# Graph layer on one core: both degree factors folded into the fp16 matrix tiles, pairs 0 and 1 prepared during the counts

## What is computed

```
h = relu(layernorm(x))                     # over the 1024 columns
avg = mean of h over the 64 images; rows normalised; sim = (avg @ avg.T + 1)/2
adj[s,d] = sim + gumbel0 > 1 - sim + gumbel1         # 0/1, 1024 x 1024
nmask = clip(adj + adj.T + I, 0, 1); common = nmask @ nmask.T
W = adj * common**2 / common.max()         # where the pair is valid
deg = W.sum(axis=0); dinv = deg**-0.5 (0 where deg is 0)
Wn = dinv[:, None] * W * dinv[None, :]
out = x + (Wn applied to h, times w) + bias          # for each image
```

## Time and profile before

| | |
|---|---|
| median of 3 runs | 912.77 us |
| profiled execution, its own time | 917.18 us |
| its span | 915.3 us |
| mean granted TensorE clock | 0.978 |
| PE busy | 846.0 us, 92% |
| VectorE (DVE) busy | 748.9 us, 82% |
| ScalarE (ACT) busy | 424.2 us, 46% |
| POOL busy | 336.9 us, 37% |

### The profile page before, as it was taken

One profiled execution on the slowest core, in us unless ns is written; L12 is line 12 of the kernel. 1 busy time (PEld: TensorE's weight loads), 2 busy tenths in 40 slices (PEclk: granted clock), 3 DMA queues, 4 the chain that ended last, 5 costly groups with the idle time before them and its releaser, 6 DMA issues.

```text
span 915.3 us, 13816 instructions
## 1 busy us (share of the span) xinstructions
PE 846.0 (92%) x4772; PEld 435.1 (48%) x4772; DVE 748.9 (82%) x792; ACT 424.2 (46%) x472; POOL 336.9 (37%) x264
## 2 busy tenths in 40 slices
PE   5999899968999999999999999999999999999997
PEld 3444455654454445444444454444444444444453
DVE  7998666888888888888888888888888888888885
ACT  3888703455444443444344444444444444444431
POOL 4788511254333333333333333333334333433330
PEclk9999899868999999999999999999999999999999
DMA  8999600040222222222222232223222222222112
GB/s 351 409 399 401 278 1 1 1 184 1 92 93 93 92 92 92 92 92 92 106 94 94 94 135 89 98 94 113 92 92 92 92 92 92 92 92 92 47 47 92
DMA packets 29108, 109.40 MB, mean 120 GB/s; under 512 B 3360, under 2 KB 3488, under 8 KB 28064
## 3 DMA queue, kind: packets, MB, share of 16 engines
q1 hardware_dynamic: 29088, 109.13, 32.3%
HBM read 75.56 MB, written 33.55 MB: 119 GB/s over the span
## 4 chain that ended last, share of the span: by engine, by line
DVE 29%; issue 27%; PE 14%; ACT 14%; POOL 13%; DVEq 1%; ACTq 1%; POOLq 1%; DMA 0%; SPq 0%
DVE zbuf L920 8%; DVE obuf L932 7%; DVE obuf L962 5%; POOL zbuf L372 5%; ACT ybuf L462 4%; PE ps L683 4%; POOL zbuf L370 4%; PE ps L650 3%; ACT hring L447 3%; ACT hring L446 3%; DVE ybuf L928 2%; DVE obuf L966 2%; PE ps L555 2%; ACT p L476 1%; PE ps L626 1%
## 5 line engine op out<-in xcount | busy, mean ns | idle before, releaser
L683 PE MATMUL ps<-a,ybuf 128*128 128x512 f16 x2688 | 598.8, 380 | 36.3 <-ACT obuf L476 29.9
L683 PEld LDWEIGHTS ps<-a,ybuf 128*128 128x128 f16 x2688 | 256.6, 98 | 357.4 <-ACT obuf L476 50.5
L462 ACT ACTIVATE ybuf<-zbuf 128x1024 f16<-128x1024 f32 (+1 forms) x128 | 121.6, 950 | 333.3 <-DVE zbuf L920 227.8
L928 DVE TENSOR_TENSOR ybuf<-zbuf,ybuf 128x1024 f16<-128x1024 f32 (+1 forms) x128 | 190.0, 1484 | 60.3 <-ACT ybuf L462 60.3
L370 POOL TENSOR_TENSOR zbuf<-zbuf 128x512 f32<-128x512 f32 x32 | 41.5, 1296 | 455.3 <-DVE zbuf L920 455.3
L850 DVE TENSOR_TENSOR hring<-hring 128x1024 f16<-128x1024 f32 x56 | 73.3, 1308 | 51.3 <-ACT hring L447 51.3
L674 PE MATMUL ps<-w,hring 128*128 128x128 f16 x1344 | 85.5, 221 | 3.6 <-DVE hring L850 3.6
L674 PEld LDWEIGHTS ps<-w,hring 128*128 128x128 f16 x1344 | 79.6, 99 | 18.4 <-DVE zbuf L920 7.4
L476 ACT ACTIVATE obuf<-ps 128x512 f32<-128x512 f32 x96 | 56.2, 586 | 64.3 <-PE ps L683 64.3
L939 DVE SCALAR_TENSOR_TENSOR obuf<-obuf,bias_sb,xring 128x1024 f32<-128x1024 f32 x64 | 82.2, 1285 | 2.9
L375 POOL TENSOR_TENSOR zbuf<-zbuf 128x512 f32<-128x512 f32 x32 | 71.8, 2244 | 0.0
(11 more groups left out here) (142 smaller groups left out, 629.6 us busy)
## 6 DMA issues: line engine op xcount, KB each, us to landing
xring<-in_x_dram SPq DMA_DIRECT2D x96, 512.0 KB, 5.0
out_dram<-obuf SPq DMA_DIRECT2D x64, 512.0 KB, 3.0
ybuf<-in_x_dram SPq DMA_DIRECT2D x28, 512.0 KB, 9.7
a<-in_L_gnn_gumbel_dram SPq DMA_DIRECT2D x7, 1024.0 KB, 14.7
obuf<-in_x_dram SPq DMA_DIRECT2D x4, 512.0 KB, 11.8
obuf<-in_L_gnn_gumbel_dram SPq DMA_DIRECT2D x1, 1024.0 KB, 22.9
w<-in_adj_dram SPq DMA_DIRECT2D x1, 64.0 KB, 1.8
bias_sb<-in_L_gnn_bias_dram SPq DMA_DIRECT2D x1, 0.5 KB, 2.1
```

Of the source, the lines that this page charges most:

```text
L462: nc.scalar.activation(y16[:, q % 2, 0, a:a + n, :], z[:, a + 1:a + 1 + n, :], ACT.Copy).then_inc(s_yhi, 1)
L683: mm = nc.tensor.matmul(bank[q % 2], y16[:, q % 2, yk, u, c * P:(c + 1) * P], a16[:, ak, mat, c, :], start=(start and c == yk == ak == 0), ...
L928: nc.vector.tensor_tensor(y16[:, q % 2, 1, a:a + n, :], z[:, a + 1:a + 1 + n, :], y16[:, q % 2, 0, a:a + n, :], ALU.subtract).then_inc(s_y, 1)
```

## The change

- **Factors.** `degree` is now the row sum of the squares of transposed masked counts: PE transposes `adjm` chunk by chunk (`turn_adj`), ScalarE copies the result out of PSUM (`turned`), VectorE multiplies the same counts with it (`mask_t`), ScalarE squares with an accumulated sum (`degree_of`). POOL raises the degrees to -1/4 (`roots`). The build multiplies the masked counts with that root of the row and of the column (`rooted`, eight tiles), and ScalarE squares with a scale `kappa` (`square`). So both factors are in the matrix, and a single factor `w_out` is left for the result.
- **Build.** t and high and low parts are now made for all four chunks of a matrix at once (2048 elements for each partition), in the order `MADE`. One of the t is POOL's (line 391). 
- **Pairs 0 and 1.** Their relu, x·W, z and y stand between the counts on all four engines. Images 1, 2 and 3 go to `obuf` as soon as `adjm` is done, the other loads of x wait for the matrices that lie in `xring`.
- **Loop.** `z_of` is a plain copy with a constant scale and moves from VectorE to ScalarE. `partial` keeps three of its four copies and adds scale and bias in them. VectorE's part is two multiply-adds for the upper halves, two for the lower and the add of x.

The diff, cut to its core:

```diff
-            sp.wait_ge(s_com, C)
-            sp.wait_ge(s_m, C)
-            for j in (1, 2, 3, 0, 4, 5, 6, 7):
+            sp.wait_ge(s_adj, C)
+            for k, j in enumerate((1, 2, 3)):
+                sp.dma_start(x_first[j], x[j]).then_inc(s_xf[k], 16)
+            sp.wait_ge(s_t, 3)
+            sp.wait_ge(s_alo, 5)
+            for j in (4, 5, 6, 7):
+                sp.dma_start(xring[:, j, :], x[j]).then_inc(s_x2[j], 16)
+            sp.wait_ge(s_alo, 6)
+            for j in (0, 1, 2, 3):
                 sp.dma_start(xring[:, j, :], x[j]).then_inc(s_x2[j], 16)
...
+            z_sums(0)
+            roots(0, 0, 6)
+            z_sums(1)
+            roots(1, 6, C)
+            pool.wait_ge(s_a32, C)
+            pool.wait_ge(s_t, 1)
+            nc.gpsimd.tensor_tensor(rows_hi[:, :, HI], rows_lo[:, :, HI], rows_hi[:, :, HI],
+                                    ALU.subtract).then_inc(s_t3, 1)
...
+            def z_of(i, q, b):
...
+                dst = z[:, 1:3, :] if b == 0 else z[:, 0:4:3, :]
+                nc.scalar.activation(dst, src, ACT.Copy, scale=Y_SCALE / W_SCALE).then_inc(s_z, 1)
...
-                nc.scalar.activation(dst, src, ACT.Copy).then_inc(s_v, 1)
+                nc.scalar.activation(dst, src, ACT.Identity, bias=bias_sb[:, 0:1],
+                                     scale=w_out[:, 0:1]).then_inc(s_v, 1)
...
+            def rooted(rows, k, c):
+                e = 2 * c + k
+                nc.vector.scalar_tensor_tensor(out=rows[:, c, :], in0=masked[e], scalar=qf[:, e:e + 1], in1=ps_q,
+                                               op0=ALU.mult, op1=ALU.mult).then_inc(s_e, 1)
...
+            def upper1(i, q):
+                r, ob = PAIRS * i + q, o[q % 2][1]
+                dve.wait_ge(s_mm, 14 + 7 * r + 5)
+                dve.wait_ge(s_v, 3 * r + 2)
+                nc.vector.scalar_tensor_tensor(out=ob[:, HI], in0=ps_b[q % 2], scalar=w_out[:, 0:1], in1=p5[:],
+                                               op0=ALU.mult, op1=ALU.add).then_inc(s_c, 1)
...
-                pe.wait_ge(s_v, 4 * r + 4)
+                pe.wait_ge(s_c, 4 * r + 10)
+                made(6)
                 product(q, 2, 6, ps_b, False)
```

More of the change, by code:

```diff
@@ L41 @@
 GUMBEL_AFTER = (1, 5, 9, 13)
-SUMMED = 3
 EPS = 1e-5
@@ L505, in _, with square @@
             y_high(0, 0, 3)
-            with act.Fori(0, TRIPS - 1) as i:
+            turned(5)
+            degree_of(4)
+            z_of(0, 1, 0)
+            y_high(0, 1, 0)
+            turned(6)
+            degree_of(5)
+            z_of(0, 1, 1)
+            y_high(0, 1, 1)
+            turned(7)
+            degree_of(6)
+            degree_of(7)
+            y_high(0, 1, 2)
+            y_high(0, 1, 3)
+            def square(rows, k, c):
+                if k == 0 and c == 0:
+                    act.wait_ge(s_kap, 3)
+                act.wait_ge(s_e, HC * k + c + 1)
+                nc.scalar.activation(rows[:, c, :], rows[:, c, :], ACT.Square,
+                                     scale=kappa[:, 0:1]).then_inc(s_a32, 1)
@@ new lines, in high @@
+            def high(mat, src):
+                nc.scalar.activation(a16[:, 0, mat, :, :], src, ACT.Copy).then_inc(s_ahi, 1)
+            for c in range(HC):
+                square(rows_hi, 0, c)
+            act.wait_ge(s_a32, HC)
+            high(0, rows_hi[:, :, LO])
+            square(rows_lo, 1, 0)
+            square(rows_lo, 1, 1)
+            act.wait_ge(s_t, 1)
+            high(3, spare)
+            square(rows_lo, 1, 2)
+            square(rows_lo, 1, 3)
+            act.wait_ge(s_a32, C)
@@ L507, in _ @@
+            with act.Fori(1, TRIPS - 1) as i:
                 for q in range(PAIRS):
@@ new lines, in _ @@
+            mask_t(0)
+            dve.wait_ge(s_cnt, 1)
+            nc.vector.tensor_scalar(w_count[:, 0:1], w_sum[:, 0:1], k0[:, 0:1], 1.0 / (A_SCALE * Y_SCALE), ALU.mult,
+                                    ALU.mult).then_inc(s_cnt, 1)
+            mask(1)
+            y_low(0, 0, 0)
+            mask_t(1)
+            h_low(0, 1, 0)
+            mask(2)
+            mask_t(2)
+            y_low(0, 0, 1)
+            mask(3)
+            mask_t(3)
+            h_low(0, 1, 1)
+            y_low(0, 0, 2)
@@ L984, in _ @@
-            low_a2(HC - 1)
-            y_low(0, 0, 2)
-            h_low(0, 1, 1)
-            y_low(0, 0, 3)
-            dve.wait_ge(s_rowp, 2)
-            nc.vector.tensor_copy(row_fb, ps_rowf).then_inc(s_rowf, 1)
-            dve.wait_ge(s_rowf, 1)
-            with dve.Fori(0, TRIPS - 1) as i:
+                lower1(i, q)
+                add_x(i, q, 1)
+            upper0(0, 0)
+            low(6, spare)
+            upper1(0, 0)
+            y_low(0, 1, 3)
+            h_low(0, 2, 0)
@@ L992, in _ @@
+            lower0(0, 0)
+            add_x(0, 0, 0)
+            h_low(0, 2, 1)
+            lower1(0, 0)
+            add_x(0, 0, 1)
+            for q in range(1, PAIRS):
+                dve_pair(0, q, True, True)
+            with dve.Fori(1, TRIPS - 1) as i:
                 for q in range(PAIRS):
```

547 lines of the change are left out of this document (297 added, 250 removed).

## The result

The changed kernel takes **877.21 us** (median of 4 runs, 875.33 to 877.45) against 912.82 for the kernel before in the same session (4 runs, 912.65 to 914.29): a ratio of 0.9602, 95% interval 0.9585 to 0.9619. That is 3.2 us over the forecast of 874 and inside the range. The profiled execution took 877.09, its span is 875.1.

A forecast was written before the change was run, and what follows sets the result against it. PE's wait before each pair's last product, from late z on VectorE, was taken to bound the loop; -44.3 (loop) + 6.5 (middle) - 0.6 (end) = -38.4 us gave 874 us, own range 868 to 882.

The forecast's parts named there:

- The loop, -44.3: Pairs 1 to 31: PE's wait before the last product goes, pairs take 20.83 or 19.49 us, 633.7 against 678.0.
- Rivals 1 and 5: Loop: last product's wait stays in part, 889 us, chance 0.16; or h_low takes 4.20 in each pair, 925 us, chance 0.03.
- Rival 1: Loop: POOL's third sum goes before h_low, upper1 ends 1.3 us later, the wait stays in part: 889 us, chance 0.16.
- The middle, +6.5: Counts, matrix build and pair 0: longer VectorE queue and PE's clock make pair 1 start at 238 against 231.5 us.
- rival 2: Counts: preparation of pairs 0 and 1 isn't covered, engines queue behind each other, 1 us per chunk: 882 us, chance 0.08.
- POOL's t: Matrix build: POOL's t of 2048 elements takes turns with VectorE, which stands some 4.5 us.
- the 2.8 us taken: Build and pair 0: loss on PE's product matmuls from the lowered clock after PE's stops, taken as 2.8 us.
- The end, -0.6: After the last matmul: one 0.75 and one add of 1.2 us, store as before, against 5.8 us now: -0.6.
- The sum: Whole kernel: -44.3 + 6.5 - 0.6 = -38.4 us, giving 874 us.
- I take the difference over to the median: Whole kernel: the profiled execution's 4.4 us above the median of 912.77 is carried into the forecast of 874.
- rival 4: Pair 0: products waiting for their matrices keep PE at 1.2 GHz, pair 1 starts 12 us later: 886 us, chance 0.07.

The follow-up runs named there:

- no_scaling: Kernel before without VectorE's two scalings of copied results with the row factor (left out of the result); z stays on VectorE: 869.29 us, ratio 0.9520.
- z_on_scalar: Kernel before with only z moved to ScalarE as a plain copy behind the x·W, factor u left out of the result: 870.14 us, ratio 0.9517.
- upper1_late2: Changed kernel with two extra reads of the same product bank in VectorE's queue just before upper1 in the loop: 878.78 us, ratio 0.9604.
- upper1_late4: Changed kernel with four extra reads of the same product bank in VectorE's queue just before upper1 in the loop: 912.71 us, ratio 0.9983.

## Why the prediction was right, and where it was off

- **The loop, -44.3.** Right: 633.7 us forecast and 633.2 found, against 677.9, so -44.7; pairs at 20.81 and 19.47, upper1 1.5 us ahead of PE (1.4 forecast). VectorE's load is 384.5 / 31 = 12.4 us per pair and ScalarE's 360.1 / 31 = 11.6, against 13 and 13. The two-pointer copies cost 0.19 us more each (772 ns where a plain copy took 586), as against 0.17. Rivals 1 and 5 did not come: h_low took 1.22 in the mean of all 56. Rival 1's premise is real, though: in a pair of no_scaling POOL's third sum went first (531.67 against 531.72), and h_low took 2.30. There the last product waits for ScalarE's copy and not for VectorE, so it cost nothing.
- **Which part brings it.** The forecast put the gain down to the change as a whole. The runs show that it is redundant: z_on_scalar or no_scaling alone reach PE's floor.
- **The middle, +6.5.** Found: pair 1 starts 2.6 us ahead of its x·W, at 236.68, against 231.55: +5.1 between the two profiled executions. 1.15 us of the difference to the forecast is no part of the change: the first stage ended that much earlier in the profile of after (turning matmul at 148.1 and 149.2). Counted from there the middle costs 6.3, next to the 6.5. By its terms: the counts ended at 181.2 (forecast 182.6), the preparation of pairs 0 and 1 was covered (rival 2 fell), and the build began at 192.3 (194). The first low part ended 15.1 us behind it (15.6). POOL's t cost VectorE 4.3 us (4.5). Not foreseen was ScalarE's queue: the third product's matrix part was done at 220.5, and PE waited until 222.4 for the copy of line 494 behind two high parts. The clock cost less than the 2.8 us taken, because most of its first part, 7.25 us for 24 matmuls, lies under that wait; what remains is 17.04 us for 72 against 15.70 at full clock, 1.3. This term depends on the execution: in upper1_late2, with the same code up to there, they took 18.61, which is 2.9 us. From the build's start to pair 1 it was 44.4 us, forecast 43.8.
- **The end, -0.6.** Right: from the last matmul to the end 5.2 us, against 5.8.
- **The sum.** -44.7 + 5.1 - 0.6 = -40.2, and the spans differ by 915.3 - 875.1 = 40.2; forecast -38.4. The medians differ by only 35.6. **The step that was off is "I take the difference over to the median"**: the profiled execution of before lay 4.4 us above its median and the one of after at its own (877.09 and 877.21). An excess of one execution is no part of what a change saves. With every term exact, that step would have given 912.8 - 40.2 = 872.6; that the forecast came nearer, at 874, is luck, for the terms were 1.8 us short the other way. 2.1 us of the excess lay ahead of the loop: no_scaling, with the same code up to pair 0's first product, is that much earlier there. The other 2.3 us do not show in the loop. no_scaling's median of 869.29, with 44.7 for the loop and 0.6 for the end, gives 914.6 for the kernel before, which had a median of 914.2 in that session and up to 915.1 in later ones. So the 912.8 of the first session was some 1.8 us low against this sum. Why is open; the changed kernel itself ran in that session alone.
- **Clock (rival 4).** The granted clock was 1.00 in the loop, as it was before with its stops of 1.4 us. The Trainium skill (TensorE: Matmul & The Clock Gate, "A second HAM failure mode: psum-queue depth-cycling") warns of a clock that swings with small idles between groups of matmuls. The loops of these runs don't show it: the granted clock is 1.00 from 245 to 860 us in every run, upper1_late4 with its 31 waits of up to 1.0 us among them. Pair 0 ran at 0.82 in the mean, not at the lower level throughout.
